# Edge windows without alignment, eleven x tiles in ring slots, and the order of the last expert steps

## What is computed

```
def gcn_conv(x, edge_index, W, b, n):
    src, dst = edge_index with a loop added at every node
    deg = segment_sum(ones, dst);  dinv = rsqrt(deg)
    h = x @ W.T
    return segment_sum(h[src] * (dinv[src] * dinv[dst])[:, None], dst) + b
x = x + gcn_conv(relu(gcn_conv(layernorm(x), W1, b1)), W2, b2)
Xn = l2norm(layernorm(x));  sp = l2norm(slot_params) * scale      # 8 experts x 4 slots
logits = Xn @ sp
D = softmax(logits over the nodes);  C = softmax(logits over the 32 slots)
H = gelu(einsum(Xn, D) @ W_down + b_down);  Y = H @ W_up + b_up
x = x + einsum(Y, C)
```

## Time and profile before

| what | value |
|---|---|
| median of 3 runs | 2862.25 us (2860.14 to 2864.53) |
| the profiled execution | 2881.27 us |
| its span, first to last instruction | 2879.6 us |
| mean granted TensorE clock | 0.867 of 2.4 GHz |
| instructions | 27437 |
| DMA | 834.62 MB, mean 290 GB/s |

### The profile page before, as it was taken

How to read it: one execution, slowest core, us unless ns; L and a number is a source line. 1 busy time by engine, 2 the same in 40 slices (tenths; PEclk the granted TensorE clock), 3 DMA queues, 4 the chain that set the end, 5 groups by cost and what they waited for, 6 DMA issues and landing times.

```text
span 2879.6 us, 27437 instructions
## 1 busy us (share of the span) xinstructions
PE 2127.8 (74%) x7723; PEld 1309.1 (45%) x7724; DVE 1723.6 (60%) x2263; ACT 531.5 (18%) x985; POOL 1683.2 (58%) x1752
## 2 busy tenths in 40 slices
PE   6615777777777777777766777778777777887768
PEld 6603444444444444444434444445444444454534
DVE  8654666655666665566645666565566656655536
ACT  7840101101111010111101111111111111111220
POOL 3246666666666666666656666666666666666300
PEclk9997898888888888988878888898888888888969
DMA  9497888888888888888868988888888888888766
GB/s 339 158 380 270 278 283 290 285 282 294 281 290 282 291 287 286 299 279 284 291 242 280 329 299 302 298 311 299 302 301 299 299 308 314 298 296 324 286 216 262
DMA packets 228816, 834.62 MB, mean 290 GB/s; under 512 B 61676, under 2 KB 62460, under 8 KB 228748
## 3 DMA queue, kind: packets, MB, share of 16 engines
q0 software_dynamic: 135968, 633.20, 63.1%
q1 hardware_dynamic: 64964, 158.63, 15.3%
q10 hardware_dynamic: 27836, 42.21, 4.0%
HBM read 784.81 MB, written 81.21 MB: 301 GB/s over the span
## 4 chain that ended last, share of the span: by engine, by line
PE 36%; issue 23%; DVE 12%; DMA 9%; POOL 9%; another core or an unknown queue 6%; ACT 3%; DVEq 1%; POOLq 0%; SPq 0%; ACTq 0%
PE work L1411 15%; PE left L1440 13%; DVE acc L1159 8%; DMA rows<-table_layer,gidx 7%; POOL rows L684 5%; POOL rows L691 3%; PE fixed L1398 2%; PE work L1426 2%; ACT logits L756 1%; ACT xsT L745 1%; PE fixed L1387 1%; DVE hot L1117 1%; PE acc L1547 1%; PE fixed L1547 1%
## 5 line engine op out<-in xcount | busy, mean ns | idle before, releaser
L1159 DVE TENSOR_TENSOR acc<-acc,rows 128x768 f32<-128x768 f32 x1078 | 1038.6, 963 | 761.5 <-DMA rows<-table_layer,gidx 534.7
L684 POOL DMA_INDIRECT rows<-table_layer,gidx x1176 | 1114.3, 948 | 359.9 <-issue 357.2
L1411 PE MATMUL work<-WT,aggT 128*128 128x384 f32 x2352 | 883.6, 538 | 250.4 <-issue 142.0
L1440 PE MATMUL left<-rows,hot 128*128 128x384 f32 x1960 | 826.7, 553 | 237.5 <-issue 235.3
L1411 PEld LDWEIGHTS work<-WT,aggT 128*128 128x128 f32 x2352 | 496.1, 213 | 642.7 <-issue 278.7
L691 POOL DMA_INDIRECT rows<-table_layer,gidx x490 | 490.4, 1001 | 484.9 <-remote 216.7
L1440 PEld LDWEIGHTS left<-rows,hot 128*128 128x128 f32 x1960 | 396.6, 214 | 512.4 <-issue 369.1
L847 ACT ACTIVATE aggT<-fixed 128x768 f32<-128x768 f32 x98 | 79.4, 810 | 1040.1 <-remote 1020.8
L815 ACT ACTIVATE acc<-rows 128x768 f32<-128x768 f32 x98 | 79.8, 815 | 822.2 <-DMA rows<-table_layer,gidx 641.6
L1398 PE MATMUL fixed<-ident,xs 128*128 128x128 f32 x294 | 68.8, 401 | 91.0 <-issue 78.0
L1398 PEld LDWEIGHTS fixed<-ident,xs 128*128 128x128 f32 x294 | 55.7, 213 | 128.1 <-issue 112.8
(11 more groups left out here) (323 smaller groups left out, 1321.1 us busy)
## 6 DMA issues: line engine op xcount, KB each, us to landing
self_row<-table_layer SPq DMA_DIRECT2D x98, 384.0 KB
rows<-table_layer,gidx POOLq DMA_INDIRECT x1666
xstage<-in_x SPq DMA_DIRECT2D x67, 384.0 KB
xs<-in_x SPq DMA_DIRECT2D x58, 384.0 KB
table_layer<-ynext SPq DMA_DIRECT2D x48, 384.0 KB
xnew<-xs SPq DMA_DIRECT2D x47, 384.0 KB
table_layer<-xstage ACTq DMA_DIRECT2D x40, 384.0 KB
rows<-xnew SPq DMA_DIRECT2D x18, 384.0 KB
```

Of the source, the lines that this page charges most:

```text
L684: pool.indirect_dma_start(rows[:, slot, :], None, table[l][0:ROWS, :], bass.IndirectOffsetOnAxis(ap=gidx[:, k % 2, slot:slot + 1], axis=0) ...
L1159: dve.tensor_tensor(acc[:, :, 0:H], acc[:, :, 0:H], halves(row), ALU.add).then_inc(S["added"], 1)
L1411: m = pe.matmul(work[:, h, 0:H], aggT[:, kc, :], WT[l][:, kc, h * H:(h + 1) * H], start=kc == 0, stop=kc == KC - 1)
L1440: m = pe.matmul(left[:, h, 0:H], hot[:, b, c, :], rows[:, slot, h * H:(h + 1) * H], start=c == 0, stop=c == LEFT - 1)
```

## The change

- The copy `src_windows` goes. POOL gathers rows of 40 edges straight from the padded edge list, with the first edge of the node as its index. The anchors, the bits and the three shifts of each part go. The four parts are 17, 16, 10 and 6 tiles instead of 13, 12, 12 and 12.
- Once the degree products are done, reloads 49 to 59 go into slots 7 to 17 of the ring `rows`, which the sweeps use later; their loads wait for no store. The other reloads wait for the stores of their own buffers as before.
- On DVE the inputs of the roots come ahead of the window indices and the coefficients right behind them; the squares of the slot parameters go ahead of the wait for the degrees.
- W_up is loaded as one of the numbered tail loads, and PE waits for it ahead of the up products instead of ahead of the fold. The two bias products come ahead of the wait for Gelu. The exponential of the second softmax moves behind all mixing weights on ACT, its division on DVE behind the copies of the fold matrix.
- The first output tile waits for one masked copy, the second for two, the third for all; the order of the three pairs of banks changes.
- The last store is made in two, of 96 rows (EVEN) and 10.

```diff
--- before.py
+++ after.py
@@ -25,9 +25,7 @@
-REACH = 48
-STEP = 8
-ANCHORS = -(-(E // STEP + 1) // P) * P
+REACH = OWN + EXTRA
@@ -43,8 +41,9 @@
+RING_X, RING_X0 = 11, 7
...
-WINDOW_PARTS = ((0, 13), (13, 25), (25, 37), (37, T))
+WINDOW_PARTS = ((0, 17), (17, 33), (33, 43), (43, T))
@@ -53,6 +52,7 @@
+EVEN = LAST // 16 * 16
@@ -90,7 +90,7 @@
-        src_windows = dram("src_windows", [ANCHORS, REACH], i32)
+        src_windows = src_pad[0:E + REACH].rearrange("(n o) -> n o", o=1)
@@ -353,7 +353,13 @@
-            return xbuf[(n if n < RELOADED else n - PARKED) % XBUFS]
+            if T <= n < T + RING_X:
+                return rows[:, RING_X0 + n - T, :]
+            return xbuf[(n if n < RELOADED else n - PARKED if n < T else n - PARKED - RING_X) % XBUFS]
+
+        def before_in_buf(n):
+
+            return n - XBUFS if n >= T + RING_X + XBUFS else n - XBUFS - RING_X
@@ -398,8 +404,7 @@
-        node_first, anchor, bit_i = (scratch[:, c:c + T].bitcast(i32) for c in (128, 192, 256))
-        bits = [scratch[:, c:c + T] for c in (320, 384, 448)]
+        node_first = scratch[:, 128:128 + T].bitcast(i32)
@@ -409,7 +414,7 @@
-        accs = [acc, fixed, left]
+        accs = [fixed, left, acc]
@@ -481,10 +486,12 @@
-                if n >= T:
-                    m = n - XBUFS - RELOADED
+                if n == T:
+                    sp.wait_ge(s["onehots_used"], GROUPS)
+                if n >= T + RING_X:
+                    m = before_in_buf(n) - RELOADED
...
-                elif n >= RELOADED + PARKED:
+                elif RELOADED + PARKED <= n < T:
@@ -506,9 +513,12 @@
-                t = n if n < LOADED else AGAIN[n - LOADED]
...
+                if n == LOADED:
+                    sp.dma_start(wup, a["W_up"].rearrange("n h d -> h n d")).then_inc(fx_in[n % 4], 16)
+                    return
+                t = n if n < LOADED else AGAIN[n - LOADED - 1]
@@ -600,15 +610,15 @@
-            sp.dma_start(wup, a["W_up"].rearrange("n h d -> h n d")).then_inc(F["w_in"], 16)
+            load_tail(LOADED)
             sp.wait_ge(F["down_done"], 1)
-            for n in range(LOADED, LOADED + KC):
+            for n in range(LOADED + 1, LOADED + 1 + KC):
...
             sp.wait_ge(F["up_done"], 1)
-            for n in range(LOADED + KC, LOADED + len(AGAIN)):
+            for n in range(LOADED + 1 + KC, LOADED + 1 + len(AGAIN)):
...
-                sp.wait_ge(f_out[b], done_count(b, 4))
+                sp.wait_ge(f_out[b], 16 * len(range(b, T + 1, 4)))
@@ -650,14 +660,14 @@
-            last_anchor = pool.to_reg(ANCHORS - 1)
-            pool.wait_ge(s["windows_out"], 16)
+            last_edge = pool.to_reg(E)
+            pool.wait_ge(s["pads_in"], 64)
...
                 for t in range(t0, t1):
-                    pool.indirect_dma_start(windows_i[:, t, :], None, src_windows[:, :],
-                                            bass.IndirectOffsetOnAxis(ap=anchor[:, t:t + 1], axis=0),
-                                            bounds_check=last_anchor, oob_is_err=False).then_inc(landed, 16)
+                    pool.indirect_dma_start(windows_i[:, t, :], None, src_windows,
+                                            bass.IndirectOffsetOnAxis(ap=node_first[:, t:t + 1], axis=0),
+                                            bounds_check=last_edge, oob_is_err=False).then_inc(landed, 16)
@@ -733,10 +743,6 @@
-            act.wait_ge(s["pads_in"], 64)
-            act.dma_start(src_windows[:, :].rearrange("(p n) w -> p n w", p=P),
-                          bass.AP(src_pad.tensor, 0, [[STEP * ANCHORS // P, P], [STEP, ANCHORS // P], [1, REACH]])
-                          ).then_inc(s["windows_out"], 16)
@@ -883,20 +889,19 @@
-                if t == THIRDS[1][1]:
-                    act.wait_ge(F["exp_in"], len(THIRDS) + 1)
-                    act.activation(cw[:, :, :], cw[:, :, :], ACT.Exp).then_inc(F["exp_done"], 1)
+            act.wait_ge(F["exp_in"], len(THIRDS) + 1)
+            act.activation(cw[:, :, :], cw[:, :, :], ACT.Exp).then_inc(F["exp_done"], 1)
...
             def store_out(t):
-                n = LAST if t == T - 1 else P
...
-                if t >= 4:
-                    act.wait_ge(f_out[t % 4], 16 * (t // 4))
-                act.dma_start(a["out"][t * P:t * P + n, :], out_buf(t)[0:n, :]).then_inc(f_out[t % 4], 16)
+                for n, (r0, r1) in enumerate(((0, EVEN), (EVEN, LAST)) if t == T - 1 else ((0, P),), t):
+                    if n >= 4:
+                        act.wait_ge(f_out[n % 4], 16 * (n // 4))
+                    act.dma_start(a["out"][t * P + r0:t * P + r1, :], out_buf(t)[r0:r1, :]).then_inc(f_out[n % 4], 16)
@@ -945,6 +950,9 @@
+            one.then(dve.tensor_tensor(aggT[:, :, 0:SLOTS], sp_c[:, :, :], sp_c[:, :, :], ALU.mult))
+            one.mark(dve.tensor_reduce(norm2_kq, aggT[:, :, 0:SLOTS].rearrange("p k (n q) -> p k q n", n=EXPERTS),
+                                       AX.X, ALU.add))
@@ -966,15 +974,20 @@
-            one.then(dve.tensor_tensor(aggT[:, :, 0:SLOTS], sp_c[:, :, :], sp_c[:, :, :], ALU.mult))
-            one.then(dve.tensor_reduce(norm2_kq, aggT[:, :, 0:SLOTS].rearrange("p k (n q) -> p k q n", n=EXPERTS),
-                                       AX.X, ALU.add))
+            dve.wait_ge(s["x_read"], T)
+            one.then(dve.tensor_scalar(recip_var[:, 0:T], ssq[:, :], 1.0 / D, LN_EPS, ALU.mult, ALU.add))
+            one.then(dve.reciprocal(recip_var[:, 0:T], recip_var[:, 0:T]))
+            dve.sem_inc(s["roots_in"], 1)
             def window_indices():
                 dve.wait_ge(s["sums_out"], 2)
...
-                one.then(dve.tensor_scalar(anchor, node_first, 3, None, ALU.arith_shift_right))
...
+                dve.wait_ge(s["roots_out"], 3)
+                one.mark(dve.tensor_copy(dinv[:, :], recip_deg))
+                one.then(dve.tensor_tensor(coef, recip_var[:, 0:T], recip_deg[:, 0:T], ALU.mult))
+                one.then(dve.tensor_tensor(shift, nmean[:, :], coef, ALU.mult))
+                dve.sem_inc(s["coef_ready"], 1)
@@ -982,19 +995,6 @@
-            dve.wait_ge(s["x_read"], T)
-            one.then(dve.tensor_scalar(recip_var[:, 0:T], ssq[:, :], 1.0 / D, LN_EPS, ALU.mult, ALU.add))
-            one.then(dve.reciprocal(recip_var[:, 0:T], recip_var[:, 0:T]))
-            dve.sem_inc(s["roots_in"], 1)
-            dve.wait_ge(s["roots_out"], 3)
-            one.mark(dve.tensor_copy(dinv[:, :], recip_deg))
-            one.then(dve.tensor_tensor(coef, recip_var[:, 0:T], recip_deg[:, 0:T], ALU.mult))
-            one.then(dve.tensor_tensor(shift, nmean[:, :], coef, ALU.mult))
-            dve.sem_inc(s["coef_ready"], 1)
-
-            for bit in range(3):
-                one.then(dve.tensor_scalar(bit_i, node_first, bit, 1, ALU.arith_shift_right, ALU.bitwise_and))
-                one.then(dve.tensor_copy(bits[bit], bit_i))
@@ -1071,17 +1071,9 @@
-                win, moved_all = windows[:, t0:t1, :], windows_tmp[:, t0:t1, :]
+                win = windows[:, t0:t1, :]
...
-                for bit in (2, 1, 0):
-                    far = 1 << bit
-                    n = OWN + EXTRA + far - 1
-                    moved = moved_all[:, :, 0:n]
-                    one.then(dve.tensor_tensor(moved, win[:, :, far:far + n], win[:, :, 0:n], ALU.subtract))
-                    one.then(dve.tensor_tensor(moved, moved, bits[bit][:, t0:t1].unsqueeze(2).to_broadcast([P, nt, n]),
-                                               ALU.mult))
-                    one.then(dve.tensor_tensor(win[:, :, 0:n], win[:, :, 0:n], moved, ALU.add))
@@ -1250,13 +1242,6 @@
-            dve.wait_ge(F["exp_done"], len(THIRDS) + 1)
-            one.then(dve.tensor_reduce(cm, cw[:, :, :], AX.X, ALU.add))
-            one.then(dve.reciprocal(cm, cm))
-            one.then(dve.tensor_tensor(cw[:, :, :], cw[:, :, :], cm.unsqueeze(2).to_broadcast([P, T, SLOTS]),
-                                       ALU.mult))
-            dve.sem_inc(F["c_ready"], 1)
-
@@ -1281,6 +1266,12 @@
+            dve.wait_ge(F["exp_done"], len(THIRDS) + 1)
+            one.then(dve.tensor_reduce(cm, cw[:, :, :], AX.X, ALU.add))
+            one.then(dve.reciprocal(cm, cm))
+            one.then(dve.tensor_tensor(cw[:, :, :], cw[:, :, :], cm.unsqueeze(2).to_broadcast([P, T, SLOTS]),
+                                       ALU.mult))
+            dve.sem_inc(F["c_ready"], 1)
@@ -1497,7 +1488,7 @@
             pe.wait_ge(F["mix_ready"], 1)
-            pe.wait_ge(F["w_in"], 16 * (EXPERTS + 3))
+            pe.wait_ge(F["w_in"], 16 * (EXPERTS + 2))
@@ -1514,9 +1505,11 @@
+            for h in range(2):
+                pe.matmul(fixed[strip_of(0), h, 0:H], sel[:, 0, :], bup[:, h * H:(h + 1) * H], start=True, stop=False)
+            pe.wait_ge(fx_in[LOADED % 4], 16 * (LOADED // 4 + 1))
             pe.wait_ge(F["gelu_done"], 1)
...
-                pe.matmul(fixed[strip_of(0), h, 0:H], sel[:, 0, :], bup[:, h * H:(h + 1) * H], start=True, stop=False)
@@ -1533,13 +1526,14 @@
```

(3 more changed lines are left out.)

4 lines of the change are left out of this document (2 added, 2 removed).

## The result

| | kernel before | changed kernel |
|---|---|---|
| median of the runs compared | 2861.19 us (2858.02 to 2864.53, 4 runs) | 2830.16 us (2824.89 to 2834.01, 4 runs) |
| profiled execution, its span | 2881.27, 2879.6 | 2834.01, 2832.3 |

What follows compares the result with a forecast made beforehand. DMA engines were read as 80 to 90% busy in nearly every slice, mostly in sweeps the diff leaves alone. From the median 2862.25, 13 us at the start and 14.2 at the end came off, giving 2835 us, range 2825 to 2846.

Steps and rivals of the forecast that it cites:

- Term 1: Ahead of the sweeps: eleven reloads issued at 117 take 4.3 MB out of the full DMA stretch, 10.5 us.
- Term 4: Start, edge lists: shorter DVE work readies them at 197, before stores end at 201.5; stores alone bind, first gather 202.7.
- the 19 us: Start: profiled execution's excess over the median, read as most late pick waits being absent from timed runs; gain taken 13, not 18.
- Rival B: Start: the late picks stand in timed runs too, so the start gives 18 us, time 2830; chance 0.15.
- Rival C: Start: six loads and six stores in flight, not bytes, set the stores' pace; start gains only 4 us, 2844; chance 0.19.
- Rival D: Window gathers on POOL's queue: each window fetched as 40 single words, 1,214 us against 65, time about 3,980; chance 0.04.
- Rival E: Sweeps eat the start's gain and the clock the end's: within 0.2%, chance 0.03; past it, 0.02.
- Term 5: Behind the sweeps: PE's fold no longer waits for W_up, 4.4 us; 3.95 after the moved output-weight operations.
- Term 6: Mixing at the end: ACT's exponential leaves its middle and W_up stops competing with last x tiles; 1.0 us, bounds 0 and 2.
- Term 7: End: bias products ahead of the activation fill only the wait for ACT, 0.65 us; products stay in PE's order.
- Term 9: Last store: split in two for row counts that use more engines, landing 2.8 us after the last addition; gains 5.8 us.
- Clock: End: PE products at 1.2 GHz may keep 2.4 GHz with shorter pauses, or not; bounds -2 and +4 us.

Runs made afterwards that it cites:

- run 5: The changed kernel itself, run again on the second chip beside the kernel before: 2853.56 us, ratio 0.9885.
- run 6: The changed kernel without ring slots, all 32 reloads waiting for the store out of their buffer again: 2860.65 us, ratio 0.9908 to the kernel before.
- run 1: The changed kernel with its six edits behind the sweeps undone, so only the start changed: 2535.64 us against 2546.0 for the kernel before, ratio 0.9961.
- run 2: The kernel before with only the six edits behind the sweeps: 2528.32 us, ratio 0.9934 to the kernel before.
- run 3: The changed kernel with 20 idle additions on VectorE behind the second part of the lists: 2525.03 us, ratio 0.9912 to the kernel before.
- run 4: The changed kernel with 20 idle VectorE additions and the second tile's picks moved ahead of them, into the lists' first part: 2518.19 us, ratio 0.989 to the kernel before.
- run 9: The changed kernel with lists made as before (expanded edge-list copy, shifts, old parts), ring slots and early coefficients kept: 2842.41 us, ratio 0.9943 to the kernel before.
- run 7: The changed kernel with W_up waited for ahead of the fold again and its load off the tail loads' counters: 2859.57 us, one execution.
- run 10: The changed kernel with old bank order, all four copies awaited before the first output, exponential and division back in the mixing: 2834.57 us, one execution.
- run 11: The changed kernel with bias products behind the activation again and the last store in one piece of 106 rows: 2840.41 us, one execution.
- run 8: The changed kernel with 22 idle products in TensorE's pauses behind the mixing: 2850.79 us, ratio 0.9882 to the kernel before.
- run 12: The changed kernel with 22 idle products, division moved behind the activation's input sum, both tiles' picks in the lists' first part: 2823.91 us, ratio 0.9872 to the kernel before.

## Why the prediction was right, and where by luck

The forecast gave 27.2 us, the measurement 31.0, and the two traces put 14.5 of it at the start and 18.6 at the end.

**Term 1, ring slots.** Right in kind, too large: 10.5 forecast; 7.3 measured in the stores' end, 6.0 at the first gather (runs 5, 6), 7.1 in the time. The step that failed is that all 4.3 MB leave the full stretch. The loads run alone only from 117 until the stores begin, and at 138 to 376 GB/s, not at 410.

**Term 2, coefficients.** 2.3 for 2.9.

**Term 3, W tile.** 0 for 0.7, at its lower bound.

**Stores together.** 12 us forecast; they end at 203.1 for 213.9 in the first traces, and on the chip without late releases at 200.7 for 211.9 (runs 1, 2): 10.8 and 11.2.

**Term 4, lists.** That the stores alone would bind failed in two ways. The second pick wait stayed whole, so the lists came at 200.8 and not at 197. And the forecast left out what VectorE still does behind them for the chunk treated apart: where the lists bind, the gather comes 4.7 us or more behind their last copy (the kernel before, runs 3, 4 and 9), which its own row of before has (215.91 to 220.59). So the first table gather came at 206.12, not 202.7. On the chip where the picks are on time it came at 201.97, with the lists' tail and the stores done within 0.1 us of each other. And the inference from the 19 us fell: most of them lay in the sweeps, not in the picks, and the waits are not a matter of profiled executions alone: in run 9 the timed runs lose the start's gain as the profile does. So the 13 stood on a wrong reading, and that it came near is luck; 14.5 with late releases and 11.1 without them is what the start is worth. Rival B's condition held, and its 2830; its 18 us did not.

**Rival C** is refuted by run 6. The dip that spoke for it comes with the late releases. **Rival D** is refuted by the packets: the gathers' packets hold 1280 bytes, 8 rows of 160. Rows that start at any edge had no price that shows: POOL's issue stays at 1.00 us, and the packets take 55 ns in the median, those of 8 aligned rows of 192 bytes 65. **Rival E** did not come.

**Term 5, W_up.** 4.4 measured, 4.7 in run 7, for 3.95. The division that was to take 0.45 of it back did so in run 5, with the down products partly at 2.4 GHz, and took nothing in the first trace, where they ran at 1.2.

**Term 6.** 1.9 in the pair of traces, but the same code spreads by 2.4 there: not settled.

**Term 7, bias.** 0.65 forecast, 2.1 measured, 1.0 to 2.1 over the runs. The step "the products themselves stay in PE's order" mis-sized it. Behind the activation each half's bias products took 1.41 us of the path at 1.2 GHz, 2.8 together. Ahead of it all four take 2.7 at 1.2 GHz, of which 2.0 stand behind the activation's end (run 5, where 1.0 was gained); in the first trace, mostly at 2.4 GHz, 1.6 and 0.9. About half of the 2.1 is therefore the clock.

**Term 8, copies.** 2.9 for 2.8, confirmed by run 10 in one execution. **Term 9, last store.** 5.7 for 5.8, confirmed by run 11 in one execution. The trace also counts what the row count does: at the end of a store of 128 rows there are 16 packets of 4 bytes, at the end of the one of 106 rows 2, and of those of 96 and 10 rows 26 together.

**Clock.** It took 1.1 in the down products. The outputs were 2.6 shorter, inside the bounds of -2 and +4, but only in part by the change: they took 66.0 us in eight of the eleven traces that have the new order of the copies, and 67.7, 68.5 and 68.6 in the other three (runs 11, 9, 3).

Most of the end's 4.4 us above its forecast came by terms 6 and 7 and the clock. At the start term 1 was over by 3 and the list chain came out too short, and the 13 was near the 14.5 because it had been cut from 18 for a reason that is false.

## What to carry to other kernels

Load into any memory that is free before the stretch that is full, but count as gain only the bytes that move before it would have begun. A reorder in a tail of short dependent stages should be costed at both clock levels, since it decides which stage runs in which. Where two chains must both be done before a stage begins, follow each to the instruction that needs it: here 4.7 us behind the last copy of the lists decided which of them bound. Before a late release is written off as a disturbance, look for the same wait throughout the trace, and on another chip.

## What the hardware showed unexpectedly

**The same program takes 2546 us on one chip and 2860 to 2887 on others**, and what differs in the traces is that TensorE's semaphores come 4 to 10 us late there, in the median of most of its lines in the sweeps, and that over 60% of the records of semaphores are missing. The Trainium skill, NOTIFIC — the notification-queue block, "7.1 Overflow: three behaviours, one of which stalls the engine", says that the block that writes the records of instructions holds the producer back when its inner buffers fill. That would fit instructions of 0.70 us on two engines at once and a release that moves by 3 us when its products move by 11. No run here shows whether it is the cause, or whether an execution without records would wait as long; it stays open, as does why one chip is free of it.

**Additions with two inputs in SBUF slow POOL's issue of gathers from 1.00 to 1.35 us** (run 3; 1.37 in the mean and once 1.50 in run 4). The kernel before has a mean of 1032 ns against 999 now; its shifts may be the cause, which no run separates. The Trainium skill, SBUF — State Buffer, "SBUF: two separate sides", has VectorE and GpSimd share a pair of ports by an exclusive lock, for VectorE's operations with two SBUF inputs as well where GpSimd's reads SBUF. The trace agrees that they collide; no gather was held for the whole of an addition, which lasts 0.79 us: it took 0.35 us longer, at most 0.50.

**Idle products kept TensorE at 2.4 GHz through part of a chain of short stages**: 2.77 us for the down products in run 8 against 4.2 to 5.3 without. They are no sure means: behind them the clock fell in the up products, and in run 12 the same ones left the down products at 4.5.
